# Wave attention: the four heads' value products in one block, one half sum moved off VectorE for two heads of four, two sines in one instruction

## The reference

```python
FREQS = [31.0, 37.0, 41.0, 43.0, 47.0]              # 16 heads of 8 channels
sim = jnp.einsum('bhid,bhjd->bhij', q, k) / sqrt(hd) / temp
scores = 0
for fi, freq in enumerate(FREQS):
    scores = scores + alpha[:, fi] * jnp.sin(TWO_PI * sim / freq + phi[:, fi])
w = jax.nn.sigmoid(scores)
w = w / (jnp.sum(w, axis=-1, keepdims=True) + 1e-10)
out = jnp.einsum('bhij,bhjd->bhid', w, v)
```

## Time and profile before

| what | value |
|---|---|
| median of 3 runs | 3736.54 us (3734.22 to 3737.48) |
| the profiled execution | 3738.18 us, span 3736.4 us |
| PE, DVE, ACT, POOL busy, of the span | 84%, 81%, 71%, 26% |
| wave attention | from about 100 us to about 1772 us of the span |

### The profile page before, as it was taken

One profiled execution on the slowest core, in us unless ns is written; L12 is line 12 of the kernel. 1 busy time (PEld: TensorE's weight loads), 2 busy tenths in 40 slices (PEclk: granted clock), 3 DMA queues, 4 the chain that ended last, 5 costly groups with the idle time before them and its releaser, 6 DMA issues. The chain is left out here.

```text
span 3736.4 us, 70767 instructions
## 1 busy us (share of the span) xinstructions
PE 3127.3 (84%) x26844; PEld 1990.0 (53%) x26844; DVE 3041.0 (81%) x4269; ACT 2656.2 (71%) x2265; POOL 981.3 (26%) x984
## 2 busy tenths in 40 slices
PE   3799999999999999998479715998998998998990
PEld 2233333333333333333358714888887887886890
DVE  8899999999999999997476545878878788786662
ACT  3899999999999999998134214776776776774430
POOL 2111111111111111110005344335245344330436
PEclk9899999999999999999679857999999999997995
DMA  5888899888999888996322227123113122112122
GB/s 163 300 332 343 335 340 346 334 337 337 345 342 340 333 343 337 341 342 253 115 74 60 55 75 183 24 32 51 28 28 51 28 36 42 28 19 74 44 61 68
DMA packets 311331, 683.36 MB, mean 183 GB/s; under 512 B 155296, under 2 KB 228608, under 8 KB 310560
## 3 DMA queue, kind: packets, MB, share of 16 engines
q1 hardware_dynamic: 302368, 661.87, 51.2%
q0 software_dynamic: 8704, 17.84, 2.0%
HBM read 90.73 MB, written 52.10 MB: 38 GB/s over the span
## 5 line engine op out<-in xcount | busy, mean ns | idle before, releaser
L758 PE MATMUL psA<-wave,diag 128*128 128x512 f32 x2560 | 1169.7, 604 | 81.5 <-DVE score L927 66.0
L827 ACT ACTIVATE wave<-wave 128x2048 f32<-128x2048 int32 x640 | 1186.8, 1908 | 44.8 <-DMA wave<-score 38.2
L758 PEld LDWEIGHTS psA<-wave,diag 128*128 128x128 f32 x2560 | 466.6, 190 | 687.7 <-issue 532.3
L880 DVE TENSOR_SCALAR score<-s,par 128x2048 int32<-128x2048 int32 x384 | 480.4, 1278 | 5.9 <-DMA wave<-score 5.8
L690 POOL TENSOR_TENSOR diag<-ident,par 128x128 f32<-128x128 f32 x384 | 143.0, 401 | 1268.7 <-PE psA L758 1268.2
L1850 POOL COPY kb<-ks 48x1024 bf16<-48x1024 bf16 x160 | 321.3, 2008 | 567.1 <-PE psR L1910 380.5
L927 DVE SCALAR_TENSOR_TENSOR score<-wave,par,score 128x1024 f32<-128x1024 f32 x384 | 469.6, 1277 | 0.0
L927 DVE SCALAR_TENSOR_TENSOR score<-wave,par,psA 128x1024 f32<-128x1024 f32 x256 | 315.6, 1274 | 46.7 <-PE psA L758 46.6
L2000 ACT ACTIVATE W<-psR 128x1024 f32<-128x1024 f32 x256 | 249.4, 1023 | 132.5 <-PE psR L1935 132.5
L1991 ACT COPY r<-psR 128x1024 f32<-128x1024 f32 x256 | 248.7, 1020 | 105.0 <-PE psR L1910 104.9
L2037 DVE TENSOR_REDUCE mx<-S 128x8 f32<-128x1024 f32 x256 | 305.4, 1214 | 2.2
(11 more groups left out here) (271 smaller groups left out, 4717.3 us busy)
## 6 DMA issues: line engine op xcount, KB each, us to landing
wave<-score SPq DMA_DIRECT2D x384, 1023.9 KB, 6.4
wave<-s SPq DMA_DIRECT2D x128, 1023.9 KB, 4.8
ks<-kb_parts SPq DMA_DIRECT2D x56, 384.0 KB, 6.1
qs<-qb_parts SPq DMA_DIRECT2D x32, 384.0 KB, 6.3
ys<-f_ys SPq DMA_DIRECT2D x36, 256.0 KB, 2.5
wave_out<-og SPq DMA_DIRECT2D x33, 256.0 KB, 7.2
o<-wave_out SPq DMA_DIRECT2D x8, 1024.0 KB, 5.3
qp<-qa_parts SPq DMA_DIRECT2D x32, 192.0 KB, 7.1
```

The costliest lines, as they stand in the source:

```text
L758: mm = pe.matmul(psA[:, kt, :], diag[:, h % 2, f, :], wave[:, h % 2, f, kt * L:(kt + 1) * L], start=(f == 0), stop=(f == PE_F - 1 or (h in ...
L827: act.activation(wave[:, h % 2, f, :], angle[:, h % 2, f, :], ACT.Sin, scale=float(TWO_PI / 2.0 ** 32)).then_inc(sine, 1)
L880: dve.tensor_scalar(out, src, scalar, par[:, u, row, h * NF + f:h * NF + f + 1], ALU.mult, ALU.add).then_inc(done, 1)
```

## The change

Three edits, all in `wave_attention`. `SPLIT_HEADS` is now heads 0 and 2, so in heads 1 and 3 TensorE adds sine 2 for both halves and VectorE's third falls away. `values` takes all four heads at once, between sine 0 and sine 1 of head 1, with the row sums of v ahead of it; the tanh of a head comes one head earlier in ScalarE's order. ScalarE computes sines 3 and 4 in one instruction over 4096 columns.

```diff
-SPLIT_HEADS = (0, 1, 2, 3)
+SPLIT_HEADS = (0, 2)
@@ credits of the semaphores
-    C_FIRST, C_VALUED, C_HALF, C_WEIGHED = 2, 4, 1, 2
+    C_FIRST, C_VALUED, C_HALF, C_WEIGHED = 2, 4, 1, 3
@@ TensorE
-            def values(g, slot, heads):
-                if heads[0] == 0:
-                    pe.wait_ge(v_ready, g + 1)
...
-                pe.wait_ge(weighed, g * HG + heads[-1] + 1)
+            def values(g, slot):
+                pe.wait_ge(v_ready, g + 1)
+                pe.wait_ge(half_ready, g + C_HALF)
...
+                pe.wait_ge(out_taken, g + C_TAKEN)
+                pe.wait_ge(weighed, g * HG + HG)
+                for kt in range(QT):
+                    for h in range(HG):
                         row = h * (P // HG)
                         mm = pe.matmul(psO[row:row + VW, :],
...
-                mm.then_inc(valued, 1)
+                mm.then_inc(valued, 2)
...
                             if more and f == 0:
                                 make_scores(n + 2, nu, nh, 1)
-                        if h in (0, 2):
-                            values(g, 1 - u, (h, h + 1))
+                            if f == 0 and h == 1:
+                                values(g, 1 - u)
@@ ScalarE
-                        for f in range(NF):
...
+                        for f in tuple(range(PE_F)) + (NF - 1,):
+                            if f == NF - 1:
+                                act.wait_ge(carried[f - 1][h % 2], (g * (HG // 2) + h // 2 + 1) * 16)
+                                act.wait_ge(cut, n * NCUT + CUTS.index(f) + 1 + C_CUT)
+                                act.activation(wave[:, h % 2, f - 1:f + 1, :].rearrange("p f n -> p (f n)"),
+                                               angle[:, h % 2, f - 1:f + 1, :].rearrange("p f n -> p (f n)"),
+                                               ACT.Sin, scale=float(TWO_PI / 2.0 ** 32)).then_inc(sine, 2)
...
-                        weigh(n - 2, (u * HG + h - 2) % AR, general)
+                        weigh(n - 1, (u * HG + h - 1) % AR, general)
```

More of the change, by code:

```diff
@@ L719, in make_scores @@
                 mm.then_inc(s_ps, 1)
-            def values(g, slot, heads):
-                if heads[0] == 0:
-                    pe.wait_ge(v_ready, g + 1)
[L724 to L729, removed]
-                pe.wait_ge(weighed, g * HG + heads[-1] + 1)
-                for kt in range(QT):
-                    for h in heads:
+            def values(g, slot):
+                pe.wait_ge(v_ready, g + 1)
+                pe.wait_ge(half_ready, g + C_HALF)
+                for kt in range(QT):
+                    mm = pe.matmul(psV[:], Vg[:, slot ^ 1, kt, :, :].rearrange("p h d -> p (h d)"),
+                                   Vg[:, slot ^ 1, kt, 0, HD:VW], start=(kt == 0), stop=(kt == QT - 1))
+                mm.then_inc(v_summed, 1)
+                pe.wait_ge(out_taken, g + C_TAKEN)
+                pe.wait_ge(weighed, g * HG + HG)
+                for kt in range(QT):
+                    for h in range(HG):
                         row = h * (P // HG)
@@ L777, in _ @@
             pair(NG // 2 - 1, True)
-            for h in (0, 2):
-                values(NG, 1, (h, h + 1))
+            values(NG, 1)
         @block.scalar
@@ L821, in pair @@
                         more = not (last and u == 1 and h >= HG - 2)
-                        for f in range(NF):
-                            if f < CARRIED:
+                        for f in tuple(range(PE_F)) + (NF - 1,):
[5 more added lines that the diff above has]
+                                               ACT.Sin, scale=float(TWO_PI / 2.0 ** 32)).then_inc(sine, 2)
+                            else:
                                 act.wait_ge(carried[f][h % 2], (g * (HG // 2) + h // 2 + 1) * 16)
[L825 to L828, removed]
+                                act.activation(wave[:, h % 2, f, :], angle[:, h % 2, f, :], ACT.Sin,
+                                               scale=float(TWO_PI / 2.0 ** 32)).then_inc(sine, 1)
                             if f in (2, NF - 1) and more:
@@ L845, in all_heads @@
                 pair(NG // 2 - 1, True, general)
-                for h in (HG - 2, HG - 1):
-                    weigh((NG - 1) * HG + h, HG + h, general)
+                weigh(NG * HG - 1, AR - 1, general)
                 outputs(NG, 1, general)
```

## The result

The changed kernel takes 3886.88 us (median of 4, 3885.38 to 3892.42) against 3735.38 of the kernel before on the same chip: a ratio of 1.0411, 95% interval 1.0393 to 1.0429. Slower, as forecast, but by 151 us where 67 were forecast, and outside the range. The profiled span is 3885.4 us, 149 more than before.

What follows compares the result with a forecast made beforehand. Bound: the handover loop between VectorE and TensorE. Steps of 15.89, 13.08, 11.47 and 13.08 make a group 53.52 against 51.43, +2.09, over 32 groups +67 us, so 3804 us; own range 3785 to 3822, widened to 3775 to 3842.

Steps and rivals of the forecast that it cites:

- The bound: In wave_attention's group loop, handover order between VectorE and TensorE sets the time; a group lasts 51.43 us.
- Four heads side by side, 3.55: TensorE's products of four heads overlap fully, so the block takes 3.55 us, as two heads took before.
- The rival of two at a time: Only two heads' products overlap, the block takes 7.10 us, the kernel 3918 us; chance 0.07.
- The place of the block counts in full: Between sine 0 and sine 1 of head 1, row sums and products add 0.87 + 3.55 = 4.42 us, unhidden.
- Step 0 to 1: From head 0's mark (start of adding sine 3 to the second half) to head 1's: 15.89 us, set by TensorE.
- The wait of VectorE for the products: Before laying down head 2's sine 3 phases, VectorE stands 1.6 us until the products have read the slot; costs 0.
- Edits 2 and 3: Sine 2 by TensorE in heads 1 and 3, 1.72 us a head; sines 3 and 4 merged, 3514 ns, gain 0.
- the tanh costs nothing: Moving the tanh one head earlier in ScalarE's order has 4.4 us to spare, so it costs 0.
- the price of sine 0 behind a wait: TensorE's eight records of sine 0 at the start of heads 1 and 3 were priced at 3.63 us.
- 2 to 3: 0.13 + 3.63 + 0.53 + 7.18 = 11.47: Mark of head 2 to head 3: handover, sine 0, two score matmuls, sixteen records of sine 1 onward; 11.47 us.
- 1.2 to spare: The DMA of head 2's sine 3 phases lands at 16.5 us after head 0's mark; ScalarE wants it at 17.7.
- The signs of being wrong: Forecast wrong if step 0 to 1 is under 14, or if VectorE and TensorE wait for ScalarE.

Runs made afterwards that it cites:

- e2: Kernel before with only heads 1 and 3 no longer split, so TensorE adds sine 2 for both halves there: 3741.87 us, ratio 1.0006.
- e7: Changed kernel, idle matmuls in TensorE's waits before heads 1 and 3, VectorE's row-sum reading after head 1, products ahead of second score matmuls: 3808.53 us.
- e1: Kernel before with only sines 3 and 4 merged into one instruction: 3734.98 us, ratio 0.9989.
- e5: Changed kernel with the block of four heads' products moved from inside head 1 to after the sums of head 0: 3744.74 us, ratio 1.0017.
- e3: Kernel before with only the four-head products block inside head 1 and the tanh one head earlier: 3891.97 us, ratio 1.0412.
- e4: Changed kernel with seven idle matmuls in TensorE's waits before heads 1 and 3, and VectorE's row-sum reading after head 1: 3867.86 us, ratio 1.0355.
- e9: Changed kernel with head 1's row sums and products ahead of the second pair of score matmuls, gaps not filled: 3921.99 us, ratio 1.0499.
- e6: e5 with seven idle matmuls in TensorE's wait before head 3 and VectorE's row-sum reading after head 1: 3742.40 us, ratio 1.0009.
- e8: e5 with only head 0 split, instead of heads 0 and 2: 3723.23 us, ratio 0.9955.
- e10: e8 with the second half of head 1's scores also copied by VectorE instead of ScalarE: 3702.80 us, ratio 0.9897.

## Why the prediction was right in direction and wrong in size

- **The bound** (a loop of handing over between VectorE and TensorE, no engine by its work): right. Steps 1 to 2 and 3 to 0 stayed at 13.1; VectorE's relief alone gave nothing (e2).
- **Four heads side by side, 3.55**: right, 864.35 to 867.90. The rival of two at a time falls. The trace agrees with the four tiles that the Trainium skill lists (TensorEngine Tiling (Array Packing), Tiling Modes). The caution about the last quadrant in the Trainium skill (TensorE: Matmul & The Clock Gate, Part 2, step 1) does not hold for this use, by the same 3.55 us.
- **The place of the block counts in full**: right. Step 0 to 1 at the full clock is 16.0 in after and 15.8 in e7, forecast 15.9. The wait of VectorE for the products was 3.41 in the group shown, forecast 1.6, because sine 0 was slow there; it was hidden as said.
- **Edits 2 and 3**: right within 5 us each (e2, e1). The price of the merged instruction was 0.1 too low. That the tanh costs nothing is not shown by a run of its own; e5 has it, with both edits, and is 4.5 us over the kernel before on its chip.
- **The step that failed is the price of sine 0 behind a wait**, the 3.63 in "0 to 1: 0.13 + 3.63 + ..." and in "2 to 3: 0.13 + 3.63 + 0.53 + 7.18 = 11.47". It is 5.33 (857.50 to 862.83). The 3.63 was read in a kernel whose waits before heads 1 and 3 were filled by products, and which had the full clock; with the products in place e2 has no low stretch in 24 groups, with only them moved e3 has 35. The text saw that the change opens these waits and counted only the idle time; that TensorE's clock may fall behind them was neither a term nor a rival, though the clock column stood in the earlier trace rows. It costs 1.7 in the step 2 to 3 in each of the 24 groups (1.5 in a few) and 0.7 on average in 0 to 1, where 10 of 24 have it: 2.4 of the 2.5 us a group by which the forecast was short. e7 shows the rest of the working to be right: its group is 53.54 against 53.52, and it is 68.7 us over the kernel before on the same chip, against 67.
- **The loop over ScalarE and the DMA** was missing as well. "1.2 to spare" was worked out for one transfer, sine 3's phases of head 2; those that come late in e4 are head 1's, queued behind the group's store and loads, and the prediction has no term for them. In after this loop lay hidden beneath the slow sine 0, and filling the gaps alone gave back 19 us of the 78 that e7 gave (3886.9 to 3867.9 and to 3808.5): two loops of nearly equal length, of which either hides the other. So the forecast would have missed its range without any fall of the clock before heads 1 and 3 too: e4 is at 3867.9, and its six low stretches are worth some 14 us of that by an estimate (1.7 each, 5.32 less 3.62, over 24 groups, so 0.4 a group). A loss of 2.4 us a group seen in a trace is thus not what its removal brings.
- **The signs of being wrong** that the prediction names did not come up, though it was wrong: 0 to 1 was not under 14, and VectorE and TensorE waited for each other above all (97.4 and 63.9 us), not for ScalarE. Neither sign looked at how long sine 0 takes.

The Trainium skill (TensorE: Matmul & The Clock Gate, A second HAM failure mode: psum-queue depth-cycling) says that short idle spells between groups of matmuls can make the clock swing between its two levels. This trace agrees: 0.83 and 1.78 us of idleness with 0.6 of work between them were followed by 1.2 GHz, in head 3 of every group and in head 1 of 10 of 24. This should have been a rival, at about +1.7 x 32 = 54 us for each of the two steps.

What stays open is when such waits let the clock fall. In after the same two waits, 0.83 and 1.77 us, stand before heads 1 and 3; before head 3 the clock fell in all of the 24 groups, before head 1 in 10. In e5 it fell in 6 of the 14 groups in which the first wait before head 3 was 0.77 to 0.84 us, and in none of the 10 in which it was shorter. The kernel before has waits of up to 1.3 us before heads 0 and 2 and one low stretch in 24 groups. The longer low stretches of e9 and e3 are open too. In e6, e7, e8 and e10, where the wait before head 3 is filled or absent, the clock did not fall in the 24 groups at all.

## What to carry to other kernels

Work that fills an engine's wait costs little where it stands (here 1.4 to 1.9 of 3.55 us); before moving it, price it where it goes, on the path from mark to mark, and ask what its old place will look like when empty. On TensorE an empty place costs more than its length, because the matmuls behind it may run at half the clock: a duration read in a kernel with full queues holds only as long as they stay full, and a few idle matmuls in a gap test this in one run, as long as no other wait takes the place of the filled one (e4). Where three engines are within a few per cent of each other, look for the second loop before believing that the removal of a wait pays.

## What the runs showed of the hardware

Matmuls of 128 x 9 weights on four row groups of the output bank overlap fully: 32 records in 3.62 us, 16 in 3.61. TensorE's clock fell after two waits of 0.8 and 1.8 us, though not each time, in a stage where TensorE was 91% busy, and adding 1.83 us of useless matmuls per gap (with the earlier reading of the row sums) made the kernel faster by 113 us (e9 to e7).
